# Routing the second expert layer inside the mixer: group by group, with fixed regions per expert

## The reference

```python
h = _layernorm(x) * (1 + ca) + sa
x = x + ga * _L1_attn_ref(h, ...)         # state-space mixer, inner width 4096, 64 heads
h = _layernorm(x) * (1 + cb) + sb
x = x + gb * _L1_ffn_ref(h, ...)
# _L1_ffn_ref: 32 experts of width 96, top 6 per token, plus a shared one of width 192
scores = jax.nn.sigmoid(x @ gate_w)
topk_w, topk_i = jax.lax.top_k(scores, 6)          # weights then divided by their sum
routed = sum over the 6 of weight * (silu(x @ wg[e]) * (x @ wu[e])) @ wd[e]
shared = silu(x @ sg) * (x @ su) @ sd
return routed + shared
```

## Time and profile before

| | us |
|---|---|
| median of 3 runs (2518.17, 2529.38, 2529.59) | 2529.38 |
| profiled execution, its own time | 2512.04 |
| its span, first to last instruction | 2510.2 |
| busy PE / DVE / ACT / POOL | 1960.5 / 1673.6 / 1452.5 / 901.4 |
| mean granted clock of TensorE | 0.882 |

### The profile page before, as it was taken

The page is one execution under the profiler, slowest core; times in us unless marked ns, Lnnn a source line. Parts: engine busy times, 40 slices in busy tenths (PEclk is TensorE's granted clock), DMA queues, the critical chain, the costliest instruction groups (busy, mean ns, idle before and its releaser), DMA issues.

```text
span 2510.2 us, 45756 instructions
## 1 busy us (share of the span) xinstructions
PE 1960.5 (78%) x12107; PEld 1604.7 (64%) x12107; DVE 1673.6 (67%) x3630; ACT 1452.5 (58%) x3953; POOL 901.4 (36%) x832
## 2 busy tenths in 40 slices
PE   4786868687469256999999999999999976049990
PEld 4565656566357245888878887888788864037770
DVE  5666756566324567888888888888888867023445
ACT  1563717364124155888878887888888851025550
POOL 0110203021343110444444444444444434755550
PEclk8897968798589677999999999999999988579995
DMA  3160573022333402444434443444344434234557
GB/s 121 51 184 18 185 200 117 18 84 87 156 100 108 137 5 85 140 150 147 147 124 147 150 149 124 143 150 150 126 143 148 150 98 129 101 114 146 155 156 247
DMA packets 168211, 319.51 MB, mean 127 GB/s; under 512 B 20176, under 2 KB 110288, under 8 KB 165776
## 3 DMA queue, kind: packets, MB, share of 16 engines
q1 hardware_dynamic: 153584, 278.31, 34.8%
q0 software_dynamic: 14496, 39.73, 4.4%
HBM read 231.68 MB, written 86.29 MB: 127 GB/s over the span
## 4 chain that ended last, share of the span: by engine, by line
PE 56%; DVE 13%; ACT 10%; issue 8%; POOL 5%; DMA 4%; PEldq 1%; DVEq 1%; ACTq 1%; PEld 1%; SPq 1%; POOLq 0%
PE bank L1741 13%; PE bank L1795 7%; PE bank L1014 5%; PE bank L1769 5%; POOL sorted_rows L1127 5%; ACT work L669 4%; PE bank L1043 3%; PE bank L1788 3%; PE bank L1781 3%; PE bank L1755 3%; DVE nmax L589 2%; PE bank L1764 2%; PE bank L998 1%; PE bank L741 1%; PEldq L142 1%
## 5 line engine op out<-in xcount | busy, mean ns | idle before, releaser
L1741 PE MATMUL bank<-h_hi,wi 128*128 128x512 f32 x1024 | 402.5, 434 | 1.0 <-ACTq L142 1.0
L1903 DVE SCALAR_TENSOR_TENSOR cv<-bank,cw,cv 128x511 f32<-128x511 f32 (+2 forms) x384 | 287.5, 749 | 84.7 <-ACT cv L1836 49.7
L1830 ACT ACTIVATE l_mat<-l_mat,cum_tok 128x128 f32<-128x128 f32 x1024 | 315.7, 429 | 0.0
L1222 DVE SCALAR_TENSOR_TENSOR experts_sg<-experts_th,bank 128x96 f32<-128x96 f32 (+2 forms) x190 | 53.8, 283 | 331.0 <-ACT experts_th L1092 330.9
L1955 POOL TENSOR_TENSOR xdec<-xdt,dec_tok 128x384 f32<-128x384 f32 x128 | 107.8, 842 | 463.7 <-DVE xdt L1893 463.7
L1970 POOL TENSOR_TENSOR yg<-yd,sgt 128x512 f32<-128x512 f32 x128 | 228.1, 1782 | 77.4 <-DVE yd L1910 77.4
L1795 PE MATMUL bank<-wo,yg 128*128 128x256 f32 x1024 | 242.4, 380 | 0.3 <-POOL yg L1970 0.3
L1131 POOL DMA_INDIRECT chosen_rows<-experts_yo,experts_xt x174 | 167.7, 964 | 191.4 <-ACT experts_yo L1099 187.5
L1741 PEld LDWEIGHTS bank<-h_hi,wi 128*128 128x128 f32 x1024 | 194.5, 190 | 62.4 <-issue 24.4
L1741 PE MATMUL bank<-h_lo,wi 128*128 128x512 f32 x512 | 202.6, 396 | 0.0
L1795 PEld LDWEIGHTS bank<-wo,yg 128*128 128x128 f32 x1024 | 184.8, 190 | 20.6 <-POOL yg L1970 0.7
(11 more groups left out here) (293 smaller groups left out, 4888.1 us busy)
## 6 DMA issues: line engine op xcount, KB each, us to landing
wi<-in_weights_split SPq DMA_DIRECT2D x128, 512.0 KB, 3.5
l_mat<-running_sums SPq DMA_DIRECT2D x128, 512.0 KB, 4.5
experts_xt<-sorted_rows SPq DMA_DIRECT2D x174, 129.0 KB, 2.1
experts_got<-chosen_rows SPq DMA_DIRECT2D x32, 512.0 KB, 8.0
wo<-out_weights_normed SPq DMA_DIRECT2D x128, 128.0 KB, 2.0
sorted_rows<-blank SPq DMA_DIRECT2D x5, 2709.0 KB, 26.6
w_raw<-in_wi SPq DMA_DIRECT2D x32, 256.0 KB, 2.6
in_weights_split<-w_hi SPq DMA_DIRECT2D x32, 256.0 KB, 2.8
```

The lines of the kernel that those rows point to most:

```text
L1741: mm = e.matmul(dst[:, :], l, r[:, k, tok], start=(n == 0), stop=(n == 3 * KD - 1))
L1830: last = e.activation(part, part, ACT.Relu, bias=cum_tok[:, c, hh, bass.ds(w.g, 1)], scale=-1.0)
L1903: e.scalar_tensor_tensor(out=cv[:, w.two, n:SEQ], in0=PSX[w.two][:, 0:SEQ - n], scalar=cw[:, bass.ds(w.f, 1), TAPS - 1 - n], in1=cv[:, w.t ...
```

## The change

What the second expert layer needs to know of a group is now computed in the mixer tiles of the group after it, one part per feature tile, and only the last group's is left for behind the mixer.

- **Fixed regions.** Each expert has a region of 17 tiles in `sorted_rows` (`DEEP`), so a row's place is `base_row` of its expert plus its rank, and groups can be placed one after another; `taken` counts what earlier groups put there. The list of 127 tiles is now a list of tile numbers (`tile_at`), which SP reads into a register for each load.
- **Blank rows.** The attention stage no longer fills all of `sorted_rows`; it writes 32 blank tiles beside it and 32 more past the regions. When the counts are known, SP copies one blank tile of 128 rows behind the last row of each expert: 32 transfers, each with an address loaded into a register.
- **Routing in pieces.** `route_pe`, `route_act`, `route_dve`, `route_pool` and `route_sync` are called at named points of a mixer step; for the three groups after the first, tiles 4 to 15 are therefore written out (`ROUTED = 3` turns of 4) on every engine, and on POOL all tiles.
- **Where the pieces stand** (part number, point of the step). PE: parts 1 to 4, two transposes; 5, eight scoring matmuls of 32 columns; 7, five ranking matmuls of up to 128 columns. ACT: 0, root and two table loads, after `cv`; 2 to 5, one modulated piece of 128 x 128 ahead of `y_off`; 6, the exponential of the scores. DVE: 0, four `bn_stats`, four `bn_aggr` and an addition, ahead of the state; 1, five for the root and four `tensor_scalar` of 256 columns; 2 to 5, one modulated piece; 6, at the end of the step, everything from the sigmoid's reciprocal to the mask, the weights and `taken`; 8, the places: a sum, four products, a reduction of 768 elements, the slots. POOL: 1 and 2, at the end of the step, two products and two sums of 128 x 512. SP: 0 and 4, at the start of the step.
- **Rows without turning back.** POOL multiplies and adds the modulation (a row in DRAM, loaded by SP after the tail) to the normalised rows. They are also kept in DRAM (`h_rows`), and the shared expert's tiles are now loaded from there, in the same buffers as the routed tiles, and turned by PE.
- **Scatters.** One per mixer tile, 24 per group, each ahead of it with its own two small copies of weight and destination; the last group's 24 run behind the mixer.

```diff
+SETS = 2 * E1
+DEEP = TOKENS // P + 1
...
+        for c in range(2):
+            for k in range(KD):
+                first = (c * KD + k) * P
+                e.dma_start(mod_rows[:, first:first + P].rearrange("b p -> p b"), mod_t[:, 1, 3 + c, k, :],
+                            allow_slow_non_contiguous=True).then_inc(s_modkept, 16)
...
+    def load_mod_row(e, r):
+        e.wait_ge(s_tailed, r + 1)
...
+        e.dma_start(mod_row[:, :, :].rearrange("p c n -> p (c n)"),
+                    mod_rows[r:r + 1, :].broadcast_to([P, 2 * D])).then_inc(s_modrow, 16)
+    def route_sync(en, r, s, at):
+        if (s, at) == (0, "a"):
+            load_mod_row(en.e, r)
+        if (s, at) == (4, "a"):
+            keep_rows(en.e, r)
+    def keep_rows(e, r):
+        e.wait_ge(*q_rowed(r + 1))
+        for n in range(2):
...
+            e.dma_start(h_rows[first:first + 2 * P, :].rearrange("(i p) d -> p i d", p=P),
+                        freed_rows[n][:, :, r, 0:D]).then_inc(s_hrows, 16)
+    def route_pe(t, r, s, at):
+        if 1 <= s <= 4 and at in "mp":
...
+        if (s, at) == (5, "p"):
...
+        if (s, at) == (7, "m"):
...
+    def route_act(a, r, s, at):
+        if (s, at) == (0, "m"):
+            e.wait_ge(*q_var(r + 1))
+            e.activation(rs[:, 1, 0:TT], rs[:, 0, 0:TT], ACT.Sqrt).then_inc(q_root.sem, 1)
+            e.activation(warm[:, 1:2], ones_c[:, :], ACT.Exp)
+        if 2 <= s <= 5 and at == "a":
...
+        if (s, at) == (6, "a"):
...
+    def route_dve(v, r, s, at):
+        if (s, at) == (0, "a"):
...
+        if (s, at) == (1, "a"):
...
+        if 2 <= s <= 5 and at == "a":
...
+        if (s, at) == (6, "z"):
+            e.wait_ge(*routed(SQUASHED, r))
+            v.step(e.tensor_scalar(scores, scores, 1.0, None, ALU.add))
+            v.step(e.reciprocal(scores, scores))
...
+            e.wait_ge(*q_rowed(r + 1))
...
+            e.tensor_copy(mask_r[:, :, :], chosen_by).then_inc(q_route.sem, 1)
...
+        if (s, at) == (8, "a"):
...
+    def route_pool(q, r, s, at):
...
+    def route_scatter(q, r, j, i):
...
+        if j:
+            e.wait_ge(*q_scat[i](16 * (TOP1 * r + j)))
+        row = row_of(r, i)
+        e.tensor_copy(row[:, D:D + 1], tw[:, r * TT + i, j:j + 1])
+        e.tensor_copy(row[:, D + 1:D + 2].bitcast(I32), tok[:, j, r * TT + i:r * TT + i + 1]).then_inc(q_meta.sem, 1)
+        e.wait_ge(*q_meta(r * (TOP1 * TT + 1) + j * TT + i + 2))
+        e.indirect_dma_start(xs[1], bass.IndirectOffsetOnAxis(slot_g[:, i, j:j + 1], 0), row, None).then_inc(q_scat[i].sem, 16)
...
+        for b in range(GROUPS + 1):
             for u in range(U):
                 run(b, 0, u)
+                if scatter and b >= 2:
+                    scatter(en, b - 2, TOP1 - 1, u)
             if b:
                 between(en, b - 1)
...
+            if b:
+                for it in range(1, 1 + ROUTED):
+                    for u in range(U):
+                        run(b, it, u, routing(b - 1, (it - 1) * U + u))
+                        if scatter and it == ROUTED:
+                            scatter(en, b - 1, 0, u)
...
+                with en.e.Fori(first, FT // U) as it:
...
+    def second_experts():
+        def sync(e, over):
...
+                else:
+                    at = e.value_load(tile_at[0:1, n - SH:n - SH + 1], min_val=0, max_val=(DEEP + 1) * NE - 1)
+                    e.dma_start(xt[:, n % LOADED, :], xs[layer].rearrange("(q p) c -> q p c", p=P)[bass.ds(at, 1), :, :]
+                                .rearrange("o p c -> p (o c)")).then_inc(s_xt[n % LOADED].sem, 16)
+            load_mod_row(e, GROUPS - 1)
+            e.wait_ge(s_hrows, 16 * 2 * (GROUPS - 1))
+            for n in range(LOADED):
+                load(n)
+            keep_rows(e, GROUPS - 1)
+            e.wait_ge(*BLANKS)
+            for k in range(NE):
+                at = e.value_load(blank_at[0:1, k:k + 1], min_val=0, max_val=DEEP * NE * P - P)
+                e.dma_start(xs[layer][bass.ds(at, P), :], blank_tiles[k * P:(k + 1) * P, :]).then_inc(s_blank[0], 16)
+            e.wait_ge(s_hrows, 16 * 2 * GROUPS)
+            for n in range(LOADED, SH):
+                load(n)
+            e.wait_ge(*LOADS_AT)
+            for i in range(TT):
+                e.wait_ge(*q_scat[i](16 * TOP * GROUPS))
+            e.wait_ge(s_blank[0], BLANK[0] + 16 * NE)
+            for n in range(SH, UNITS_ALL):
+                load(n)
```

More of the change, by code:

```diff
@@ L1283, in program @@
     NC, NB, U, BACK = TT, GROUPS * FT, 4, 4
+    freed = ExitStack()
+    freed_rows = [sb(f"freed_rows{n}", [P, KD, GROUPS, SEQ], where=freed) for n in range(2)]
+    freed.close()
     h_hi = sb("h_hi", [P, KD, TOKENS], F32R, where=mix)
@@ L1324, in program @@
     sq = sb("sq", [P, SEQ], where=stream)
-    warm = sb("warm", [P, 1], where=stream)
+    warm = sb("warm", [P, 2], where=stream)
+    mod_row = gates[:, 0, 0:2, :]
     m_mat = outs[:, :, :].rearrange("p (s h) t -> p s h t", s=2)
@@ L1348, in program @@
             "sums_turned", "bc_products", "sums_split", "last_sums", "last_sums_used", "decays", "start_out", "products_masked")]
+    (q_var, q_root, q_rows, q_turned, q_ht, q_route, q_rowed, q_tw, q_slot, q_meta) = [signal(n, count) for n, count in (
+        ("variance", GROUPS), ("root", GROUPS), ("rows", GROUPS), ("turned", KD * TT * GROUPS),
+        ("modulated", KD * TT * GROUPS), ("routing_handed_on", 4 * GROUPS + 4), ("rows_back", GROUPS),
+        ("weights_of_top", GROUPS), ("slots", GROUPS), ("meta", (TOP1 * TT + 1) * GROUPS))]
@@ new lines, in program, with routed, turned_at, freed_tile @@
+    q_scat = [signal(f"scattered{i}", 16 * TOP1 * GROUPS) for i in range(TT)]
+    s_modrow, s_hrows = sem("modulation_row_in"), sem("modulated_rows_kept")
+    SCORED, SQUASHED, MASKED, RANKED = 1, 2, 3, 4
+    routing_bank, ranking_bank = [bank[n][:, 3 * P:4 * P] for n in (5, 6)]
+    def routed(what, r):
+        return q_route(4 * r + what)
+    def turned_at(r, n):
+        return (ranking_bank, routing_bank)[n % 2] if r < GROUPS - 1 else bank[n][:, 0:P]
+    def freed_tile(r, i):
+        return freed_rows[i // 2][:, i % 2, r, :]
@@ L1515, in start_dve @@
         e = v.e
+        v.own.add(e.memset(taken[:, 0, :], 0.0))
         e.wait_ge(s_ssm, SSM_IN)
@@ L1662, in __init__ @@
             f = u - back
-            if first and f < 0:
-                b, f = b - 1, f + FT
+            if first:
+                f += it * U
+                if f < 0:
+                    b, f = b - 1, f + FT
             self.b, self.live = b, 0 <= b < GROUPS
@@ L1671, in __init__, with nothing, mixer_stream, run @@
             self.end = first and f == FT - 1
-            self.begun = first and b == 0
-    def mixer_stream(en, step, between):
-        def run(b, it, u):
-            step(en, [Tile(b, it, u, back) for back in range(BACK + 1)])
-        for b in range(GROUPS):
+            self.begun = first and b == 0 and f < U
+    ROUTED = 3
+    def nothing(at):
+        pass
+    def mixer_stream(en, step, between, piece, scatter=None):
+        def run(b, it, u, route=nothing):
+            step(en, [Tile(b, it, u, back) for back in range(BACK + 1)], route)
+        def routing(r, s):
+            return lambda at: piece(en, r, s, at)
+        for b in range(GROUPS + 1):
             for u in range(U):
                 run(b, 0, u)
+                if scatter and b >= 2:
+                    scatter(en, b - 2, TOP1 - 1, u)
             if b:
                 between(en, b - 1)
-            with en.e.Fori(1, FT // U) as it:
-                for u in range(U):
-                    run(b, it, u)
-        for u in range(U):
-            run(GROUPS, 0, u)
-        between(en, GROUPS - 1)
+            if b == GROUPS:
+                break
+            if b:
[4 more added lines that the diff above has]
+                            scatter(en, b - 1, 0, u)
+            first = 1 + (ROUTED if b else 0)
+            if scatter and b:
+                for it in range(first, FT // U):
+                    for u in range(U):
+                        run(b, it, u)
+                        scatter(en, b - 1, it - ROUTED, u)
+            else:
+                with en.e.Fori(first, FT // U) as it:
+                    for u in range(U):
+                        run(b, it, u)
     def mixer_sync(e, over):
@@ L1712, in mixer_sync, with step @@
         e.wait_ge(g_masked, GROUPS + 1)
-        def step(_, tiles):
+        def step(_, tiles, route):
+            route("a")
             w = tiles[0]
@@ L1727, in step, with mixer_pe_step @@
                             .rearrange("o p n -> p (o n)")).then_inc(s_wo[w.two], 16)
-        mixer_stream(Engine(e, "sync", None), step, lambda en, b: None)
-    def mixer_pe_step(t, tiles):
+        mixer_stream(Engine(e, "sync", None), step, lambda en, b: None, route_sync)
+    def mixer_pe_step(t, tiles, route):
         e = t.e
@@ L1779, in mixer_pe_step @@
             e.wait_ge(s_xdec, done(w.g))
+            route("m")
```

(4 more changed lines are left out.)

458 lines of the change are left out of this document (441 added, 17 removed).

## The result

| | before | after |
|---|---|---|
| median of 9 runs each | 2524.52 | 2541.41 |
| ratio, 95% interval | | 1.0079 [1.0053, 1.0104] |
| the same pair on two other chips | | 1.0105 [1.0091, 1.0120], 1.0130 [1.0111, 1.0148] |
| profiled execution, span | 2510.2 | 2532.3 |

The three pairs give 17, 26 and 35 us more. The forecast was 2529, no change; 2541 is inside its range, on the side of the rival in which SP becomes the bound (2546).

A forecast was written before the change was run, and what follows sets the result against it. It took a ring through DVE's taps and ACT to bound the mixer, and POOL's 96 row scatters the stretch behind it. Sum 58.5 - 62.5 + 5 - 1.5 = -0.5 us, so 2529; range 2495 to 2556.

The forecast's parts named there:

- SP becomes the bound: Rival, behind the mixer: register load 0.8, 1.25 per blank transfer, every routed return 0.1 late; +17, 2546 us; chance 0.15.
- A: Mixer, change of groups: SP issues modulation row and fifth tile's weights only after the tail, delaying PE; +6.2 us per group.
- B: Mixer, normalising on DVE: five small instructions and four of 256 columns, less 0.45 idle; +2.0 us per group.
- C and D: Mixer, turning, scoring and ranking: four ACT pieces 1.1 us, PE's added work 1.4; together +2.5 us per group.
- E: Mixer, top-k and mask in one step: nearly thirty DVE instructions, ACT's exponential, PE's low clock; +7.5 us per group.
- F: Mixer, computing the slots on DVE: 2.5 less 0.45 idle, +2.0 us per group.
- G: Mixer, ninth tile: SP waits for POOL's rows and issues two 512 KB writes before the weights; +2.5 us per group.
- H: Mixer, twelve tiles per group written out instead of looped: 7.71 instead of 8.06 us each, -4.2 us per group.
- J: Mixer: POOL's row operations meet two-input DVE operations; between 0 and 2, taken +1.0 us per group.
- Gain survives: Rival: SP's register load nearly free, 0.5 per blank transfer, PE doesn't stop, tile loop untouched; -33.6, 2496 us; chance 0.2.
- the row isn't queued: Rival, behind the mixer: modulation row lands by 2060, not behind the weights, routing ends earlier; -17.5, 2512 us; chance 0.12.
- DVE loses the port: Rival, mixer: scatters cost 0.25 each beyond idle time beside DVE's two-input work, normalising 1.9; +24, 2553 us; chance 0.13.

The follow-up runs named there:

- e8_loads_first: Changed kernel with SP's modulation row and kept rows moved behind the mixer's loads of steps 2 and 6; ratio 0.9998 to the kernel before, mixer 1117.7 us.
- e7_before_unrolled: Kernel before the change with all 32 mixer tiles of a group written out, no routing in them; ratio 0.9894 to the kernel before, mixer 1049.5 us.
- e9_weights_by_act: Changed kernel with the second layer's ten expert weight loads issued on ScalarE's queue instead of SP's; ratio 0.9970 to the kernel before.
- e1_twice: Changed kernel with 32 more address reads and 32 more constant-address transfers on SP behind the blank transfers; ratio 1.0279 to the kernel before.
- e3_row_first: Changed kernel with the last group's modulation row loaded ahead of the ten weight loads; ratio 1.0050 to the kernel before.
- e10_five_together: Changed kernel with weights on ScalarE's queue, shared loads between blanks, read ahead, SP's mixer steps late, all mixer tiles written out; 2452.42 us, ratio 0.9696 to before.
- e12_all_written_out: Changed kernel with the mixer tiles that four engines still looped over written out too; ratio 1.0021 to the kernel before, mixer 1125.3 us.
- e14_changed_third: The changed kernel unaltered, run again as reference with a third profile; 2547.54 us, ratio 1.0130 to the kernel before.

## Why the prediction was wrong

It said no change, with SP at 0.95 per blank transfer, and gave 0.15 to the case that came. The profiles' means differ by 28.2 us where the sum said -0.5. Of these 28.7, 13.6 are the routed tiles, 7.3 the time to the first routed product, 6.9 the mixer; the last 0.9 are stages before and after, and the -1.5 for PE's start, which no run shows by itself. By its own steps:

- **The failed step: SP's register read, taken as "hidden in the usual tile" (+5 for the routed tiles) and as part of the "0.95 per transfer, between both" of the blanks.** I bounded a register read on SP by PE's pauses, 0.32 in the mean and 0.8 at most, and chose near the mean of a pause in which something else hid part of the read. On SP the read is 0.55, the bare transfer 0.64, not 0.45, and 0.14 more come with an address in a register.
- **Routed tiles.** +18.6 instead of +5, outside the bound of 13. The place was right ("in that return path"), the size wasn't: with the read ahead of the wait the loop is 221.5 and 222.9, with it inside 232.1 to 241.7, so it is not hidden. The ring's eighth gives 12.5 of the 18.6; the rest it does not explain. The prediction named this as a sign of being wrong: the time from the first routed tile to the end, 282.6 before, is 295.9, 305.0 and 303.6.
- **Blanks.** 1.3 to 1.4 per transfer, beyond my upper bound of 1.25: 41 to 45 us instead of 30.4. PE's stop is 19.4 to 25.1 at the ninth shared tile, as named, instead of 15.5, and behind it the products of a shared tile take 2.77 instead of 1.46 (granted clock 0.50 in those 4 us, 1.00 in the next). First routed product 49 to 63 earlier, mean 55.2, instead of 62.5.
- **Mixer.** 58.5 forecast, 65.4 measured. The prediction counts from 7.71 and takes twelve tiles for written out; in `yd` periods over the 8.06 of a loop tile, mean of three groups, with the forecast brought to the same base in brackets, it is: A +6.0 (5.9), B +2.1 (1.7), C and D +4.3 (0.8), E +7.0 (7.2), F and G together +2.5 (4.2).
  - *C and D* are the term that was mis-sized, by 3.5 per group. `e8_loads_first` takes 2.6 of it back, so that much was SP's two steps, felt in later tiles than at the boundary, and not turning and scoring.
  - *H* is 0.24 per tile, not 0.35: 7.71 belongs to four written-out tiles between two register loops, where the earlier trace rows stand; next to other written-out tiles the same four take 7.82 to 7.83 in `e7_before_unrolled`.
  - *G* was wrong as a mechanism: the ninth tile is no shorter with the rows kept later, and the two writes are 256 KB each (256 rows of 256 numbers), not 512, and land in 2.2 to 2.9 us.
  - *J* was about right: beside POOL's row operations five of VectorE's products for the decayed matrix take 1.64 in the mean instead of 1.22, 2.1 us in three groups where +3 was forecast.
- **Row behind the weights.** Forecast 46.7 after the mixer; POOL had it 43.0 after, in the other two profiles 43.9 and 34.9. Right, but I took the landing time as fixed, and it makes 9 of the 12.5 us by which one execution's head is shorter than another's (the blanks took 4 us less too).
- **Rivals.** "SP becomes the bound" forecast -53, +13 and 2546; -55.2, +18.6 and 2541 came, and its turning point, 1.1 per transfer, is passed. Its name says too much all the same: a second read in each of the 127 tiles cost 9 to 19 us, not the 70 that they would if SP were the pace. "Gain survives" is out by 1.31 per transfer; "the row isn't queued" by the 43.0 us, and `e9_weights_by_act` shows that it is the queue; "DVE loses the port" by the 7.82 of tiles with scatters. The sentence on the Trainium skill (DMA: Bandwidth & Descriptors, section Latency and other measured facts) gave about 600 ns for a `tensor_load`; the trace has 0.27 for that instruction and 0.55 with the register arithmetic behind it. The estimate from it, 1.05 per transfer, was nearer to the measured 1.31 than my 0.95.

What stays open: why the tile loop takes 232 to 242 us with the read inside, between executions of one kernel too, while the two with the read ahead differ by 1.4 and three without a read by 2.9 (215.6 in `e7_before_unrolled`); why a loss of 18.5 comes where the ring's eighth gives 12.5; and why written-out tiles take 7.71 in some places and 7.82 in others.

## What to carry to other kernels

Count an address in a register as an instruction chain on the engine that issues the transfer, and put the read ahead of the wait, never between a wait and the transfer that it frees. When small transfers are added to a queue, look at what is queued ahead (megabytes of weights hold data and issuing engine alike) and at what is queued behind (shared loads behind 32 blanks). Another order or another engine's queue can be had for little: here ten issues on ScalarE held its own first work back by some 6 us and still paid. Sizes read at a special place, as at a change of stages, are not those of the steady stretch.

## What the runs showed of the hardware

- A register read from SBUF on SP costs 0.55 us in a row of 32 (`e1_twice`); a 129 KB transfer to a constant address 0.64, the pair with the address in the register 1.33.
- SP's issues stand still while its queue holds weights: eight loads of 128 KB took 20.1 us (`e3_row_first`) to 33.0 (`e8_loads_first`), against 3.8 to 5.3 with the queue free (`e9_weights_by_act`, `e10_five_together`, and the last eight in the changed kernel).
- A mixer tile in a register loop takes 8.06 us, the same tile written out 7.82, with constants in place of registers for its addresses: 3% of a tile (`e7_before_unrolled`, `e12_all_written_out`).
- The time after which a small transfer was through 9 MB of weights varied from 34.9 to 48.0 us between ten profiles (`e14_changed_third`, `e8_loads_first`).
